# A new order of the relative attention on all engines, and attention weights split by GpSimd alone

## The reference

```python
h = L0_tok(x)                                   # 64 x 25 x 192
h = concat([cls_tok, h])                        # 64 x 26 x 192
h = h + L0_attn(layernorm(h)); h = h + L0_ffn(layernorm(h))   # low-rank q, k, v; 32 experts
h = h + L1_attn(layernorm(h)); h = h + L1_ffn(layernorm(h))   # relative attention; 8 experts
h = h + L2_attn(layernorm(h)); h = h + L2_ffn(layernorm(h))   # performer; block with 4 experts
h = h + L3_attn(layernorm(h)); h = h + L3_ffn(layernorm(h))   # quantised input; routed block
```

```python
qkv = (x @ qkv_w.T)
attn = einsum('bhqd,bhkd->bhqk', q, k) * scale
attn = attn + einsum('bhqd,qkd->bhqk', q, tab_kv[iv] + tab_kh[ih]) * scale
attn = softmax(attn)
out = einsum('bhqk,bhkd->bhqd', attn, v) + einsum('bhqk,qkd->bhqd', attn, tab_vv[iv] + tab_vh[ih])
out = out.reshape(b, n, 768) @ proj_w.T + proj_b
```

## Time and profile before

| | |
|---|---|
| runs | 3562.09, 3571.14, 3571.66 us; median 3571.14 |
| the profiled execution | 3562.04 us; its span 3560.1 us |
| TensorE (PE) busy | 3168.9 us, 89% of the span |
| VectorE (DVE) busy | 2382.9 us, 67% |
| ScalarE (ACT) busy | 1209.3 us, 34% |
| GpSimd (POOL) busy | 645.9 us, 18% |
| granted clock of TensorE, mean | 0.923 of full speed |

### The profile page before, as it was taken

How to read it: one execution, slowest core, us unless ns; L and a number is a source line. 1 busy time by engine, 2 the same in 40 slices (tenths; PEclk the granted TensorE clock), 3 DMA queues, 4 the chain that set the end, 5 groups by cost and what they waited for, 6 DMA issues and landing times. The chain is left out here.

```text
span 3560.1 us, 61301 instructions
## 1 busy us (share of the span) xinstructions
PE 3168.9 (89%) x21505; PEld 2958.7 (83%) x21505; DVE 2382.9 (67%) x5919; ACT 1209.3 (34%) x2419; POOL 645.9 (18%) x733
## 2 busy tenths in 40 slices
PE   6779999999999999999699789998979889676587
PEld 5669999999999999999688779997758779665476
DVE  2657677777777777777577557775457557796666
ACT  2333333333333333333333233333445333233233
POOL 1111111111111111111211111111223111121220
PEclk8779999999999999999899879999989879887698
DMA  2010000000000000000000000000000000000000
GB/s 96 1 47 32 32 31 31 31 28 25 28 30 31 31 31 31 31 31 0 34 2 2 32 17 31 32 16 9 1 10 17 32 16 17 9 1 3 12 16 15
DMA packets 9707, 82.40 MB, mean 23 GB/s; under 512 B 1285, under 2 KB 1541, under 8 KB 3194
## 3 DMA queue, kind: packets, MB, share of 16 engines
q1 hardware_dynamic: 9466, 79.59, 6.1%
HBM read 78.29 MB, written 1.30 MB: 22 GB/s over the span
## 5 line engine op out<-in xcount | busy, mean ns | idle before, releaser
L716 ACT ACTIVATE hid<-bank,dat 128x384 f32<-128x384 f32 (+1 forms) x1104 | 671.6, 609 | 1402.2 <-PE bank L446 1273.8
L685 PE MATMUL bank<-w,hid_hi 128*128 128x384 f32 x3588 | 1038.1, 361 | 0.0
L687 PE MATMUL bank<-w,hid_lo 128*128 128x192 f32 x3588 | 901.6, 251 | 0.0
L687 PEld LDWEIGHTS bank<-w,hid_lo 128*128 128x128 f32 x3588 | 686.4, 191 | 1.9
L748 DVE TENSOR_TENSOR hid_lo<-hid,hid_hi 128x384 fp32r<-128x384 f32 (+1 forms) x1104 | 653.4, 592 | 38.4
L685 PEld LDWEIGHTS bank<-w,hid_hi 128*128 128x128 f32 x3588 | 673.7, 188 | 1.9
L745 DVE CAST hid_hi<-hid 128x384 fp32r<-128x384 f32 (+1 forms) x1104 | 412.8, 374 | 174.6 <-ACT hid L716 173.1
L759 DVE SCALAR_TENSOR_TENSOR h_tok<-bank,gate,h_tok 128x192 f32<-128x192 f32 x520 | 216.7, 417 | 318.9 <-PE bank L687 312.3
L446 PE MATMUL bank<-xa_hi,w_hi 128*128 128x384 f32 (+1 forms) x1104 | 401.7, 364 | 9.9 <-DVEq L1747 5.6
L446 PE MATMUL bank<-xa_hi,w_lo 128*128 128x384 f32 (+1 forms) x1104 | 393.9, 357 | 0.0
L446 PE MATMUL bank<-xa_lo,w_hi 128*128 128x384 f32 (+1 forms) x1104 | 393.8, 357 | 0.0
(11 more groups left out here) (296 smaller groups left out, 4376.0 us busy)
## 6 DMA issues: line engine op xcount, KB each, us to landing
raw<-in_L_exp SPq DMA_DIRECT2D x44, 1344.0 KB, 5.7
pix<-in_pixels SPq DMA_DIRECT2D x6, 832.0 KB, 9.2
wp_raw<-in_L_att SPq DMA_DIRECT2D x1, 2880.0 KB, 9.3
raw<-in_L_mlp SPq DMA_DIRECT2D x2, 1344.0 KB, 6.4
wp_raw<-in_L_att SPq DMA_DIRECT2D x2, 768.0 KB, 4.2
tok<-in_tok SPq DMA_DIRECT2D x1, 1248.0 KB
out<-h_tok SPq DMA_DIRECT2D x1, 1248.0 KB, 4.4
wp_raw<-in_L_fat SPq DMA_DIRECT2D x1, 960.0 KB, 4.9
```

Of the source, the lines that this page charges most:

```text
L685: nc.tensor.matmul(o[:, 0:2 * D], hid_hi[k % 2][:, m, c], w2[j][:, m, :], start=m == 0, stop=False)
L687: ins = nc.tensor.matmul(o[:, 0:D], hid_lo[k % 2][:, m, c], w2[j][:, m, 0:D], start=False, stop=m == HC - 1)
L716: nc.scalar.activation(hid[(6 * k + m) % 3][:, 0:128 * nt], bank[4 + (6 * k + m) % 4][:, 0:128 * nt], func, bias=bias).then_inc(s["h_act"] ...
```

## The change

It has five parts.

1. Relative attention: `order` and `dve_order` are new. Values of a turn's first tile now come ahead of the next turn's k, the first tile of the next turn is normalised within the current turn, and VectorE takes a shift and a normalise of each tile in turn.
2. Weights of at most 2304 columns (`NARROW`): GpSimd casts as well as subtracts; ScalarE has no part in it.
3. Weights of the relative attention: two loads, of one third and of two thirds, the second issued after the first has landed. GpSimd casts the first third and subtracts the first and the second; ScalarE casts the last third, then the middle one; VectorE subtracts the last.
4. First attention: its weights are loaded at the start of the program; the ten low-rank matmuls stand at the head of the features phase, two to a bank in banks 3 to 7; ScalarE copies them out in five copies of 128x384 ahead of the second block's tiles.
5. The expert weights behind the relative attention are loaded after tile 14's values, not after tile 13's.

```diff
@@ features_phase
             def tensor(pe):
+                if products:
+                    products["tensor"](pe)
                 for i, (t0, n) in enumerate(TBLK):
+                    if products and i in (1, 2):
+                        products["kept"](pe, 1 if i == 1 else 5)
...
                     normalise(0)
                     root(2)
+                    if products:
+                        products["scalar"](act)
                     normalise(1)
@@ attention_weights
+            ON_POOL, ON_ACT = (cols, cols) if cols <= NARROW else (cols // 3, cols * 2 // 3)
+            shared = ON_POOL < cols
...
             def sync(sp):
-                sp.wait_ge(s["phase_done"].sem, 3 * after)
+                if after:
+                    sp.wait_ge(s["phase_done"].sem, 3 * after)
...
+                elif shared:
+                    sp.dma_start(wp_raw[:, 0:ON_POOL], a[cfg.dram][:, 0:ON_POOL]).then_inc(s["att_in"].sem, 16)
+                    sp.wait_ge(s["att_in"].sem, b["att_in"] + 16)
+                    sp.dma_start(wp_raw[:, ON_POOL:cols], a[cfg.dram][:, ON_POOL:cols])\
+                        .then_inc(s["att_in"].sem, 16)
...
+            def products(pe):
                 pe.wait_ge(s["att_in"].sem, b["att_in"] + 32)
-                pe.wait_ge(s["lo_full"].sem, b["lo_full"] + 4)
                 for m in range(5):
                     f = (0, 0, 1, 1, 2)[m]
                     for k in range(2):
-                        n = 2 * m + k
-                        if n >= 4:
-                            pe.wait_ge(s["job_used"].sem, b["job_used"] + n - 3)
-                        nc.tensor.matmul(bank[n % 4][:, 0:D], low[:, 256 * f + 128 * k:256 * f + 128 * k + 128],
+                        ins = nc.tensor.matmul(bank[3 + m][:, D * k:D * k + D],
...
             def scalar(act):
-                for m in range(5 if low_rank else 0):
...
-                nc.scalar.activation(wp_hi[:, 0:cols], wp_raw[:, 0:cols], ACT.Identity)\
-                    .then_inc(s["att_hi"].sem, 1)
+                act.wait_ge(s["att_in"].sem, b["att_in"] + 32)
+                for c0, c1 in ((ON_ACT, cols), (ON_POOL, ON_ACT)):
+                    nc.scalar.activation(*high(c0, c1), ACT.Identity).then_inc(s["att_hi"].sem, 1)
+
+            def vector(dve):
+                dve.wait_ge(s["att_hi"].sem, b["att_hi"] + 1)
+                nc.vector.tensor_tensor(*low_part(ON_ACT, cols)).then_inc(s["att_ready"].sem, 1)
...
-                pool.wait_ge(s["att_hi"].sem, b["att_hi"] + 1)
-                nc.gpsimd.tensor_tensor(wp_lo[:, 0:cols], wp_raw[:, 0:cols], wp_hi[:, 0:cols].bitcast(F32),
-                                        ALU.subtract).then_inc(s["pool_step"].sem, 1)
+                pool.wait_ge(s["att_in"].sem, b["att_in"] + (32 if low_rank else 16))
+                if low_rank:
+                    pool.wait_ge(s["job_used"].sem, b["job_used"] + 5)
+                nc.gpsimd.tensor_copy(*high(0, ON_POOL)).then_inc(s["pool_step"].sem, 1)
                 pool.wait_ge(s["pool_step"].sem, b["pool_step"] + 1)
-                nc.gpsimd.memset(pads[-2], 0.0).then_inc(s["att_ready"].sem, 1)
+                ins = nc.gpsimd.tensor_tensor(*low_part(0, ON_POOL))
+                if shared:
+                    pool.wait_ge(s["att_hi"].sem, b["att_hi"] + 2)
+                    ins = nc.gpsimd.tensor_tensor(*low_part(ON_POOL, ON_ACT))
+                ins.then_inc(s["pool_step"].sem, 1)
@@ attention
-                order = [("k", 0, 1), ("bd", 0, 0), ("mass", 0, 0), ("q", 0, 1), ("scores", 0, 1), ("values", 0, 0),
-                         ("v", 0, 1), ("out", 0, -1), ("bd", 1, 0), ("mass", 1, 0), ("exp", 0, 1), ("scores", 1, 1),
-                         ("values", 1, 0), ("v", 1, 1), ("back", 0, -1), ("exp", 1, 1)]
-                dve_order = [("normalise", 0, 0), ("split", 0, -1), ("spread", 0, 1), ("normalise", 1, 0),
-                             ("shift", 0, 1), ("shift", 1, 1), ("back", 0, -1)]
+                order = [("values", 0, 0), ("k", 0, 1), ("bd", 1, 0), ("q", 0, 1), ("v", 0, 1), ("mass", 1, 0),
+                         ("scores", 0, 1), ("values", 1, 0), ("exp", 0, 1), ("v", 1, 1), ("out", 0, -1), ("bd", 0, 1),
+                         ("mass", 0, 1), ("scores", 1, 1), ("exp", 1, 1), ("back", 0, -1)]
+                dve_order = [("normalise", 1, 0), ("split", 0, -1), ("spread", 0, 1), ("shift", 0, 1),
+                             ("normalise", 0, 1), ("back", 0, -1), ("shift", 1, 1)]
@@ the phases
-        load, split, w = expert_weights(8, a["L1_exp"], ("av_full", signals["av_full"].at + 2 * 14))
+        load, split, w = expert_weights(8, a["L1_exp"], ("av_full", signals["av_full"].at + 2 * 15))
```

More of the change, by code:

```diff
@@ L942, in attention_weights, with high, low_part @@
             low_rank = cfg.low_rank
[L943 to L944 removed]
+            ON_POOL, ON_ACT = (cols, cols) if cols <= NARROW else (cols // 3, cols * 2 // 3)
+            shared = ON_POOL < cols
+            b = base(att_in=32 if low_rank or shared else 16, att_hi=2 * shared, att_ready=1 + shared,
+                     pool_step=2, job_full=5 * low_rank, job_used=5 * low_rank)
             n, QW = 4 * cfg.G * SLOT, 4 * cfg.G * SLOT + 8
[L947 to L948 removed]
+            pads = [xs[:, p, :, :].rearrange("p j (m s) -> p (j m) s", s=32)[:, :, SLOT:32] for p in range(3)]
+            pads += [p[:, :, SLOT:32] for p in p_t] + [v_x[:, :], rel_a[:, :, 20:32]]
+            q_pads = q_t[:, 0:cfg.no_q * QW].rearrange("p (c n) -> p c n", n=QW)[:, :, n:QW]
+            def high(c0, c1):
+                return wp_hi[:, c0:c1], wp_raw[:, c0:c1]
+            def low_part(c0, c1):
+                return wp_lo[:, c0:c1], wp_raw[:, c0:c1], wp_hi[:, c0:c1].bitcast(F32), ALU.subtract
             def sync(sp):
[L951 removed]
+                if after:
+                    sp.wait_ge(s["phase_done"].sem, 3 * after)
                 if low_rank:
@@ L998, in attention_weights, with products_kept @@
-            return dict(sync=sync, tensor=tensor, scalar=scalar, gpsimd=gpsimd)
+                        ins = nc.tensor.matmul(bank[3 + m][:, D * k:D * k + D],
+                                               low[:, 256 * f + 128 * k:256 * f + 128 * k + 128],
+                                               low[:, 768 + D * m:768 + D * m + D], start=True, stop=True)
+                    ins.then_inc(s["job_full"].sem, 1)
+            def products_kept(pe, m):
+                pe.wait_ge(s["job_used"].sem, b["job_used"] + m)
@@ new lines, in keep_products @@
+            def keep_products(act):
+                for m in range(5):
+                    act.wait_ge(s["job_full"].sem, b["job_full"] + m + 1)
+                    dst = wp_raw[:, 0:2 * cfg.C].rearrange("p (k c) -> p k c", k=2)[:, :, D * m:D * m + D]
+                    nc.scalar.activation(dst, bank[3 + m][:, 0:2 * D].rearrange("p (k c) -> p k c", k=2),
+                                         ACT.Identity).then_inc(s["job_used"].sem, 1)
+            def scalar(act):
+                act.wait_ge(s["att_in"].sem, b["att_in"] + 32)
+                for c0, c1 in ((ON_ACT, cols), (ON_POOL, ON_ACT)):
+                    nc.scalar.activation(*high(c0, c1), ACT.Identity).then_inc(s["att_hi"].sem, 1)
@@ L1000, in attention @@
+            parts = dict(sync=sync, gpsimd=gpsimd)
+            if shared:
+                parts.update(scalar=scalar, vector=vector)
+            return parts, dict(tensor=products, scalar=keep_products, kept=products_kept)
         def attention(cfg, res, *others):
@@ L1685, in vit_tower @@
         conv_phase()
-        features_phase(n_tok, attention_weights(l0, 1), norm_of=h_tok)
+        weights, products = attention_weights(l0, 0)
+        features_phase(n_tok, weights, norm_of=h_tok, products=products)
         load, split, w = expert_weights(32, a["L0_exp"], scores_done())
@@ L1715, in vit_tower @@
         add_phase(h_tok, y_tok)
-        norm_phase(h_tok, n_tok, attention_weights(l3a, len(phases)))
+        norm_phase(h_tok, n_tok, attention_weights(l3a, len(phases))[0])
         quantise_phase(n_tok)
@@ L1725, in vit_tower @@
         route_phase()
-        phases.append(attention_weights(l3f, len(phases)))
+        phases.append(attention_weights(l3f, len(phases))[0])
         load, split, w = expert_weights(1, a["L3_mlp"], scores_done())
```

29 lines of the change are left out of this document (9 added, 20 removed).

## The result

The change makes the kernel slightly slower: 3580.86 us (median of 9 runs, 3574.40 to 3586.32) against 3571.14 (9 runs, 3562.09 to 3576.51), ratio 1.0032 with a 95% interval of 1.0020 to 1.0045. The forecast was 3581.0. The sum came out; two of its terms did not, and they had opposite signs.

A forecast was written before the change was run, and what follows sets the result against it. The prediction took TensorE to bound stage R, the experts being untouched; +18.2 us there and -8.1 for the splits gave +10.1, put on the median of 3571.14 as 3581 us, range 3558 to 3593.

The forecast's parts named there:

- Stage R: Relative attention of the second layer, 1736.75 to about 2043.5 us before the change; taken as bound by TensorE.
- closed chain: Steady turns of stage R: shifts, normalises and scores wait on each other over VectorE, ScalarE and TensorE; sum 35.6 us.
- ScalarE's branch: Stage R turns: ScalarE copies its block before draining q; 6.2 us in place of 5.5 for split and spread.
- Its size, +18.2 us: Stage R: 101.1 us for the ends plus six turns of 37.3, 324.9 against 306.7 us; bounds +12.2 and +24.2.
- A clock of 0.87 in the turns: Stage R turns: granted clock 0.87 puts 13% of TensorE's 11 us at half rate, +1.4 us less gaps, turn 37.3.
- GpSimd holds VectorE's scale steps: Feature and norm phases: small VectorE steps wait for GpSimd's running instruction; splits sum to -8.1 us, without hold -28.7.
- First attention, -7.7 us: Ahead of the first attention: TensorE starts at 64.1, not 71.8, one scale step held; without the hold -10.9 us.
- Sum: Whole kernel: +18.2 for stage R and -8.1 for the splits make +10.1 us; on the median 3581 us.
- (b): Rival, feature and norm phases: GpSimd does not hold VectorE, -28.7 us there, total -17 to -11; chance 0.1.
- (a): Rival, stage R: it gets no slower or gains, total -6 to 0 us; chance 0.15.
- (c): Rival, stage R: clock falls to 0.80, turns of 39 us, stage +28, total +20 us; chance 0.1.
- (d): Rival, stage R: loads still land late, would need 8 us more to matter; no chance of its own.

The follow-up runs named there:

- the order alone: Kernel before the change with only the new relative-attention lists and the later expert load: 3591.45 us, ratio 1.0063.
- the two halves: Kernel before with only the new relative-attention order, ratio 1.0063; the change with the old order, so splits and low-rank products only, ratio 0.9966.
- the order with q around the mass: Kernel before with four of six q products ahead of the first tile's mass, two behind, and values ahead of scores: 3543.66 us, ratio 0.9932.
- the new order with q early: Kernel before with the new relative-attention order, but ScalarE copies q out ahead of the weights' blocks: 3579.32 us, ratio 1.0040.
- the spread first: Kernel before with the new relative-attention order, q copied ahead of the blocks, and VectorE spreading k before the split: 3574.51 us, ratio 1.0019.
- the kernel whose GpSimd waits: The change with the old relative-attention order, GpSimd waiting for the last scale step of its phase: 3538.86 us, ratio 0.9925 to the kernel before.

## Why the forecast was right, and where it was not

- **Stage R is slower because of a closed chain.** Right, and shown: with ScalarE's branch taken out the turn fell to 35.36 us (the chain over VectorE was added up to 35.6), with the split out of the chain by another 1.64, to 33.72, where 2.3 was its length.
- **Its size, +18.2 us.** Too small; the traces have +27.6 and the runs of the order alone about +22. The start was 80.85 us to the first split and not 78.6, six turns 226.1 and not 223.8, the end 27.5 and not 22.5. The end is the term missed most. The prediction gives it without its pieces. TensorE waited 6.9 us just ahead of it, for the last mass, and the granted clock in it was 0.74: the last output's 36 matmuls took 7.4 us (from 2056.66), the same 36 of the output before 4.3 (from 2047.89), and three of the six groups of the last values' matmuls ran at about half rate, 1.3 us a group and not 0.7. Together that is some 5 us, about what was missed.
- **A clock of 0.87 in the turns.** It was 0.93, as in the turns before the change; what the stage lost of its clock (0.89 against 0.92) it lost in its start and its end. The turn came out right within 0.4 us since the other part, the wait behind the block copies, was larger than the 0.7 us set down for it: taking the branch out gave 2.3 us a turn, and VectorE's wait for the relative scores was 7.39 us and not 3.5 to 4.5. (The prediction says that 0.87 puts 13% of the work at half rate; it is about a quarter of the time, which costs the 13% that it counts.)
- **GpSimd holds VectorE's scale steps.** Right at three of four places to 0.15 us: -3.3 (-3.29), +0.4 (+0.54), and +2.5 for both norm phases with the hold of the phase behind given back (+0.09, +2.51).
- **First attention, -7.7 us.** It was -10.95, the bound without a hold: the last scale step ended 0.07 us ahead of the subtraction instead of falling into it.
- **Sum.** +9.4 missed in stage R and -3.3 in the first attention left +16.5 by the traces. The median showed +9.7, as the two halves measured alone: +22 of the order is 5 less than the traces' stage, within its interval. The agreement with 3581.0 is thus owed in part to chance; that the sign and the range held is owed to the chain and the hold.
- **Rivals.** No hold (b) and no slower stage R (a) are out. (c) has nearly the stage's number, +28 against +27.6 in the traces, but not its mechanism: it had the turns at a clock of 0.80 and 39 us, and they had 0.93 and 37.68, while the rest was lost in the stage's start and end. (d) is out: stage R starts the 3.3 us earlier that were forecast.

## What to carry to other kernels

Before two steps are interleaved on an engine, follow one turn as a closed chain over all engines, and count how long the first turn and the last one stand alone: here the start cost 21 to 25 us, the end gave back 4, and the turns, at best 2.2 us shorter, could not pay for the rest. A step handed to an engine that shares something with the bottleneck belongs where the other runs only instructions that are not held, and each place it is moved to has to be looked at again, since the hold moves with it. Where the bottleneck engine waits, put independent work of its own there: four products put ahead of a 2 us wait, with the values behind it, gave 24 us, twice what the splits of the change gave.

## What the runs showed of the hardware

A wait of TensorE can cost more than its length. In stage R the order with q around the mass took 1.9 us of waiting out of a turn, and the turn got 3.6 us shorter (35.94 to 32.38), at a granted clock of 0.99 instead of 0.93. What goes with the clock in these turns is the long single wait and not the sum of the waits. The six turns before the change and those of the new order with q early:

```profile
1796.14:2011.80 215.66, 193.56 (x2304) 186.39 (x2304) 152.15 (x539) 75.25 (x186) 29.49 (x60) 0.93 0.04 14
1823.83:2036.02 212.19, 186.15 (x2293) 174.35 (x2292) 151.20 (x539) 71.71 (x185) 28.16 (x57) 0.99 0.03 12
```

TensorE is idle for (215.66 - 193.56) / 6 = 3.7 us a turn in the first and (212.19 - 186.15) / 6 = 4.3 in the second, which has the higher clock. In the first, five of the six turns have one wait of 1.9 to 2.0 us; in the second the longest is 1.35. The other traces fall on the same two sides: 0.93 to 0.97 where such waits stand, 0.99 to 1.00 in the five kernels without them. No run varies the length of the wait alone.

Behind the stage, in the 135 us that begin 15 us after it, the clock was 0.94 instead of 0.89 in both kernels with q around the mass, and the experts were 5.7 to 5.8 us shorter. A high clock in the turns is not enough for that: with the spread first they had 0.99, and the stretch behind had 0.89 and 412.34 us. And the old order had 0.93 and 407.96 there in the kernel whose GpSimd waits. What decides it is not shown.

Unchanged stretches differed between executions. In the 13 traces the first attention took 177.4 us twice, 179.2 and 179.9 once each and 181.2 to 182.1 otherwise, the first experts 1455.7 to 1455.8 four times and 1458.3 to 1458.7 otherwise, the third layer 407.5 to 413.3. A comparison of two single traces of this kernel is uncertain by about that much.
